# Two cross-attention layers on one core: scores in fp32 in place of three split products, and the last stage's root mean square moved into the clamp of the query lengths

## The reference

```python
def layer0(x, y, ...):
    xn, yn = layernorm(x, ln1_w, ln1_b), layernorm(y, ln2_w, ln2_b)
    q = (xn @ Wq)                       # 16 heads of 16
    k, v = split(yn @ Wkv)
    attn = softmax(q k^T * 16 ** -0.5)
    x = x + (attn v) @ Wproj + bproj
    h = gelu(layernorm(x, ln3_w, ln3_b) @ W1 + b1)
    return x + h @ W2 + b2
def layer1(x, enc, norm_w, wq, wkv, wout):
    xn = x * rsqrt(mean(x * x, -1) + 1e-5) * norm_w
    q = rotate(xn @ wq);  k, v = split(enc @ wkv);  k = rotate(k)
    q = q / maximum(norm(q), 1e-12);  k = k / maximum(norm(k), 1e-12)   # per head
    attn = softmax(q k^T * sqrt(16))
    return x + (attn v) @ wout
```

## Time and profile before

| | us |
|---|---|
| three runs | 385.35, 385.97, 391.71 |
| median | 385.97 |
| span of the profiled execution | 386.9 |

### The profile page before, as it was taken

One profiled execution on the slowest core, in us unless ns is written; L12 is line 12 of the kernel. 1 busy time (PEld: TensorE's weight loads), 2 busy tenths in 40 slices (PEclk: granted clock), 3 DMA queues, 4 the chain that ended last, 5 costly groups with the idle time before them and its releaser, 6 DMA issues.

```text
span 386.9 us, 11499 instructions
## 1 busy us (share of the span) xinstructions
PE 356.5 (92%) x4475; PEld 318.7 (82%) x4475; DVE 294.4 (76%) x654; ACT 239.3 (62%) x464; POOL 197.1 (51%) x177
## 2 busy tenths in 40 slices
PE   8998999999999989898999999978889989989974
PEld 5977888888888867798999998978778878878854
DVE  4799987989899773267755559467899999999752
ACT  2356677666677655815644476163877777777862
POOL 2474544554665611003331233248899998999810
PEclk9999999999999999999999999999999999999999
DMA  6853001110000000000000000000001001010001
GB/s 157 246 158 121 27 25 43 32 28 25 2 3 4 22 2 2 2 2 0 0 0 0 0 0 3 10 22 0 22 12 36 26 26 42 29 37 14 29 30 41
DMA packets 14432, 12.39 MB, mean 32 GB/s; under 512 B 2996, under 2 KB 13752, under 8 KB 14392
## 3 DMA queue, kind: packets, MB, share of 16 engines
q1 hardware_dynamic: 14384, 11.83, 10.4%
q10 hardware_dynamic: 8, 0.00, 0.0%
HBM read 9.73 MB, written 2.10 MB: 31 GB/s over the span
## 4 chain that ended last, share of the span: by engine, by line
PE 58%; issue 22%; DVE 10%; ACT 5%; POOL 4%; POOLq 0%; DVEq 0%; ACTq 0%
PE bank_qk L697 9%; PE banks_s L745 6%; PE bank_y L834 4%; PE bank_y L828 3%; PE banks_s L1032 3%; PE bank_t L800 3%; PE bank_qk L722 3%; PE bank_o L736 3%; PE bank_t L697 3%; PE bank_qk L726 3%; DVE row_max L1203 2%; POOL x_all L375 2%; PE bank_y L1052 2%; PE bank_o L1021 2%; PE bank_y L929 1%
## 5 line engine op out<-in xcount | busy, mean ns | idle before, releaser
L413 POOL TENSOR_TENSOR norm_inv<-norm_sq_min,minus_half 128x32 f32<-128x32 f32 x16 | 87.5, 5468 | 1.8 <-DVE norm_sq_min L1374 1.8
L576 ACT ACTIVATE W_s<-banks_s,b_cols 128x256 f32<-128x256 f32 x60 | 25.0, 469 | 41.3 <-PE banks_s L915 41.3
L342 POOL TENSOR_TENSOR masked<-qkT_r,halves_t 128x512 fp32r<-128x512 f32 x32 | 32.9, 1050 | 24.1 <-DVE qkT_r L1193 24.1
L477 ACT ACTIVATE PT<-banks_s 128x1024 f32<-128x1024 f32 x32 | 31.0, 1022 | 20.3 <-PE banks_s L782 18.3
L1203 DVE TENSOR_REDUCE row_max<-banks_s 128x8 f32<-128x1024 f32 x32 | 37.6, 1218 | 7.7 <-PE banks_s L745 7.7
L368 POOL TENSOR_TENSOR b_var_eps<-b_mean_var,eps_t 128x2 f32<-128x2 f32 x8 | 1.6, 197 | 69.1 <-DVE b_mean_var L1137 69.1
L915 PE MATMUL banks_s<-lnT_hi,W_hi 128*128 128x256 f32 x120 | 34.2, 285 | 0.0
L915 PE MATMUL banks_s<-lnT_hi,W_lo 128*128 128x256 f32 x120 | 33.9, 283 | 0.0
L915 PE MATMUL banks_s<-lnT_lo,W_hi 128*128 128x256 f32 x120 | 33.9, 283 | 0.0
L642 ACT ACTIVATE PT<-banks_s 128x1024 f32<-128x1024 f32 x32 | 31.1, 1024 | 4.1 <-PE banks_s L1032 4.1
L745 PE MATMUL banks_s<-masked,qkT_r 32*128 32x256 f32 x768 | 31.5, 294 | 1.6 <-DVE row_max L1203 1.3
(11 more groups left out here) (171 smaller groups left out, 1095.6 us busy)
## 6 DMA issues: line engine op xcount, KB each, us to landing
ctx_in<-in_ctx SPq DMA_DIRECT2D x32, 96.0 KB, 2.0
x_all<-in_x SPq DMA_DIRECT2D x16, 128.0 KB, 2.1
W_s<-in_L_xattn_W SPq DMA_DIRECT2D x2, 1024.0 KB, 6.4
out<-Wq_s SPq DMA_DIRECT2D x16, 128.0 KB, 1.8
Wq_s<-in_L_xattn_Wq SPq DMA_DIRECT2D x1, 256.0 KB, 3.0
Wkv_s<-in_L_xattn_Wkv SPq DMA_DIRECT2D x1, 256.0 KB, 3.2
Wproj_s<-in_L_xattn_Wproj SPq DMA_DIRECT2D x1, 256.0 KB, 4.2
wout_s<-in_L_xattn_wout SPq DMA_DIRECT2D x1, 256.0 KB, 3.0
```

Of the source, the lines that this page charges most:

```text
L342: nc.gpsimd.tensor_tensor(masked[:, r, 1, :, half, :], qkT_r[:, r, 1, :, :].bitcast(fp32), ones, ALU.mult)\
L413: nc.gpsimd.tensor_tensor(norm_inv[:, j, :], norm_sq_min[:, j, :], minus_half[:, :], ALU.pow)\
L477: nc.scalar.activation(PT[:, 2 * h:2 * h + 2, :], banks_s[:, 2 * h:2 * h + 2, :], ACT.Exp, scale=HD ** -0.5)\
L576: last = nc.scalar.activation(hT[:, m, :], (bank or bank_s[u])[:, 256 * k:256 * k + 256], ACT.Gelu, bias=b1_cols[:, m:m + 1])
```

## The change

- Queries and keys of both attention stages are kept as one fp32 copy (qkT, masked). score_terms and scores issue one fp32 product where three fp32r products stood: 8 per call in place of 24.
- The low parts go: queries_keys_lo, masked_lo, units_lo. In stage A the two masks are shared: ACT makes the one for the first half (masked_act), POOL the one for the second (masked_pool). In stage C ACT makes all three copies (units_out).
- In stage C x isn't normalised any more. inputs_c turns x_all itself. The mean square, scaled by EPS_L2 ** 2, is the lower limit in the clamp of the query lengths; keys keep the constant. POOL's power of it goes, and so do DVE's multiplication and rms_inv.
- New waits: mean_square on POOL's sum of two tiles before, POOL's sum on the clamp of two tiles before, the query clamp on POOL's sum, inputs_c on b_x (the MLP's residual) in place of norm_done. normed_c, units_T and scores wait for ACT's c_unit_T where they waited for DVE's c_unit_lo.
- TensorE's steps of stage C are all written out.

```diff
@@ -107,14 +107,15 @@
         minus_half = sb("minus_half", 128, 2 * H)
+        clamp_eps = sb("clamp_eps", 128, 1)
         x_all = sb("x_all", 128, NB, C1)
...
         inT = sb("inT", 128, 2, 4, TOK)
-        qkT_r = sb("qkT_r", 128, RING, 2, 4, TOK, dtype=fp32r)
-        masked = sb("masked", 128, RING, 2, 4, 2, TOK, dtype=fp32r)
-        pair = masked[:, :, :, 0:KT, :, :]
+        qkT = sb("qkT", 128, RING, 4, TOK)
+        masked = sb("masked", 128, RING, 4, 2, TOK)
+        pair = masked[:, :, 0:KT, :, :]
         vals = sb("vals", 128, 2, H, VW)
@@ -331,38 +332,37 @@
-            def masked_lo(t):
+            def masked_pool(t):
...
                     r = t % RING
-                    pool.wait_ge(a_qk_lo, t + 1)
+                    pool.wait_ge(a_qk_ready, t + 1)
                     wait(pool, a_shifted, t - 2)
-                    for half in range(2):
+                    for half in (1,):
                         ones = halves_t[:, half:half + 1].unsqueeze(2).broadcast_to([128, 4, TOK])
-                        nc.gpsimd.tensor_tensor(masked[:, r, 1, :, half, :], qkT_r[:, r, 1, :, :].bitcast(fp32), ones, ALU.mult)\
-                            .then_inc(a_masked_lo, 1)
+                        nc.gpsimd.tensor_tensor(masked[:, r, :, half, :], qkT[:, r, :, :], ones, ALU.mult).then_inc(a_masked_pool, 1)
@@ -400,16 +400,14 @@
                     pool.wait_ge(C["stats_ready"], t + 1)
-                    nc.gpsimd.tensor_tensor(mean_sq_eps[:, j, :], mean_sq[:, j, :], eps_t[:, 0:1], ALU.add)\
+                    wait(pool, c_norm_min, 2 * t - 2)
+                    nc.gpsimd.tensor_tensor(mean_sq_eps[:, j, :], mean_sq[:, j, :], clamp_eps[:, :], ALU.add)\
                         .then_inc(C["var_ready"], 1)
-                    pool.wait_ge(C["var_ready"], t + 1)
-                    nc.gpsimd.tensor_tensor(rms_inv[:, j, :], mean_sq_eps[:, j, :], minus_half[:, 0:1], ALU.pow)\
-                        .then_inc(C["rstd_ready"], 1)
...
                 if ok(t):
-                    pool.wait_ge(c_norm_min, t + 1)
+                    pool.wait_ge(c_norm_min, 2 * t + 2)
                     nc.gpsimd.tensor_tensor(norm_inv[:, j, :], norm_sq_min[:, j, :], minus_half[:, :], ALU.pow)\
@@ -438,21 +436,20 @@
-            def queries_keys_hi(t):
+            def queries_keys_T(t):
...
                     wait(act, a_shifted, t - 2)
-                    nc.scalar.activation(qkT_r[:, t % RING, 0, :, :], bank_qk[:, :].rearrange("p (a b) -> p a b", a=4), ACT.Copy)\
-                        .then_inc(a_qk_hi, 1)
-
-            def masked_hi(t):
-
-                if ok(t):
-                    act.wait_ge(a_qk_hi, t + 1)
-                    for half in range(2):
-                        nc.scalar.activation(masked[:, t % RING, 0, :, half, :], qkT_r[:, t % RING, 0, :, :].bitcast(fp32),
-                                             ACT.Copy, scale=halves_t[:, half:half + 1]).then_inc(a_masked_hi, 1)
+                    nc.scalar.activation(qkT[:, t % RING, :, :], bank_qk[:, :].rearrange("p (a b) -> p a b", a=4), ACT.Copy)\
+                        .then_inc(a_qk_ready, 1)
+
+            def masked_act(t):
+
+                if ok(t):
+                    act.wait_ge(a_qk_ready, t + 1)
+                    nc.scalar.activation(masked[:, t % RING, :, 0, :], qkT[:, t % RING, :, :], ACT.Copy, scale=halves_t[:, 0:1])\
+                        .then_inc(a_masked_act, 1)
@@ -597,7 +594,8 @@
                     wait(act, C["stats_ready"], t)
-                    nc.scalar.activation(x_sq[:, :], tile_of(t), ACT.Square, scale=C1 ** -0.5, accum_out=mean_sq[:, j, :])\
+                    wait(act, C["var_ready"], t - 1)
+                    nc.scalar.activation(x_sq[:, :], tile_of(t), ACT.Square, scale=EPS_L2 * C1 ** -0.5, accum_out=mean_sq[:, j, :])\
                         .then_inc(C["stats_ready"], 1)
@@ -622,16 +620,16 @@
-            def units_hi(t, j):
+            def units_out(t, j):
...
                     for half in range(2):
-                        nc.scalar.activation(pair[:, j, 0, :, half, :], bank_o[:, 0:C1].rearrange("p (a b) -> p a b", a=KT),
-                                             ACT.Copy, scale=halves_t[:, half:half + 1]).then_inc(c_unit_hi, 1)
-                    nc.scalar.activation(qkT_r[:, j, 0, KT:, :], bank_o[:, C1:].rearrange("p (a b) -> p a b", a=KT), ACT.Copy)\
-                        .then_inc(c_unit_hi, 1)
+                        nc.scalar.activation(pair[:, j, :, half, :], bank_o[:, 0:C1].rearrange("p (a b) -> p a b", a=KT),
+                                             ACT.Copy, scale=halves_t[:, half:half + 1]).then_inc(c_unit_T, 1)
+                    nc.scalar.activation(qkT[:, j, KT:, :], bank_o[:, C1:].rearrange("p (a b) -> p a b", a=KT), ACT.Copy)\
+                        .then_inc(c_unit_T, 1)
@@ -740,18 +738,17 @@
                 for tile in range(KT):
-                    for n, (a, b) in enumerate(HI_LO):
-                        for g in range(QUARTERS):
-                            last = mm(bank_s[g][:, 2 * TOK * tile:2 * TOK * (tile + 1)], qkT_r[quad(g), r, a, rows + tile, :],
-                                      masked[quad(g), r, b, columns + tile, :, :], start=n == 0 and (stop or tile == 0), stop=stop and n == 2)
-                            if stop and tile == KT - 1 and n == 2:
-                                last.then_inc(A["scores"], 1)
+                    for g in range(QUARTERS):
+                        last = mm(bank_s[g][:, 2 * TOK * tile:2 * TOK * (tile + 1)], qkT[quad(g), r, rows + tile, :],
+                                  masked[quad(g), r, columns + tile, :, :], start=stop or tile == 0, stop=stop)
+                        if stop and tile == KT - 1:
+                            last.then_inc(A["scores"], 1)
...
                 if ok(t):
-                    pe.wait_ge(a_masked_hi, 2 * t + 2)
-                    pe.wait_ge(a_masked_lo, 2 * t + 2)
+                    pe.wait_ge(a_masked_act, t + 1)
+                    pe.wait_ge(a_masked_pool, t + 1)
                     wait(pe, a_maxed, 2 * t)
@@ -985,11 +982,11 @@
                 if ok(t):
-                    pe.wait_ge(C["norm_done"], t + 1)
+                    pe.wait_ge(b_x, upto(t + 1))
                     pe.wait_ge(c_loaded[j], LOADED * (nth + 1))
...
                     for k in range(KT):
-                        nc.tensor.transpose(bank_t[:, 128 * k:128 * k + 128], xn[:, j, 128 * k:128 * k + 128], ident[:, :])
+                        nc.tensor.transpose(bank_t[:, 128 * k:128 * k + 128], tile_of(t)[:, 128 * k:128 * k + 128], ident[:, :])
                     for k in range(2):
@@ -1024,15 +1021,14 @@
                 if ok(t):
-                    pe.wait_ge(c_unit_lo, t + 1)
+                    pe.wait_ge(c_unit_T, 3 * t + 3)
                     wait(pe, C["exped"], 2 * t)
                     for half in range(KT):
-                        for n, (k, q) in enumerate(HI_LO):
-                            for g in range(NG):
-                                last = mm(bank_s[g][:, 2 * TOK * half:2 * TOK * (half + 1)], qkT_r[quad(g), j, k, KT + half, :],
-                                          pair[quad(g), j, q, half, :, :], start=n == 0, stop=n == 2)
-                                if half == KT - 1 and n == 2:
-                                    last.then_inc(C["scores"], 1)
+                        for g in range(NG):
+                            last = mm(bank_s[g][:, 2 * TOK * half:2 * TOK * (half + 1)], qkT[quad(g), j, KT + half, :],
+                                      pair[quad(g), j, half, :, :], start=True, stop=True)
+                            if half == KT - 1:
+                                last.then_inc(C["scores"], 1)
@@ -1056,7 +1052,7 @@
                     pe.wait_ge(C["on_ready"], t + 1)
-                    pe.wait_ge(c_unit_lo, upto(t + 3))
+                    pe.wait_ge(c_unit_T, 3 * upto(t + 3))
                     wait(pe, c_onT_lo, t)
@@ -1106,7 +1102,7 @@
             scores(0, 0)
-            pipeline(pe, step_c, 4, STEPS_C, peeled=8)
+            at(step_c, *range(4, STEPS_C))
@@ -1371,7 +1347,10 @@
                     dve.wait_ge(c_norm_sq, t + 1)
-                    v.tensor_scalar(norm_sq_min[:, j, :], norm_sq[:, j, :], EPS_L2 ** 2, None, ALU.max).then_inc(c_norm_min, 1)
+                    v.tensor_scalar(norm_sq_min[:, j, H:], norm_sq[:, j, H:], EPS_L2 ** 2, None, ALU.max).then_inc(c_norm_min, 1)
+                    dve.wait_ge(C["var_ready"], t + 1)
+                    v.tensor_scalar(norm_sq_min[:, j, 0:H], norm_sq[:, j, 0:H], mean_sq_eps[:, j, 0:1], None, ALU.max)\
+                        .then_inc(c_norm_min, 1)
@@ -1185,14 +1181,6 @@
-            def queries_keys_lo(t):
...
-                    v.tensor_tensor(qkT_r[:, r, 1, :, :], bank_qk[:, :].rearrange("p (a b) -> p a b", a=4),
-                                    qkT_r[:, r, 0, :, :].bitcast(fp32), ALU.subtract).then_inc(a_qk_lo, 1)
@@ -1334,13 +1317,6 @@
```

(31 more changed lines are left out.)

52 lines of the change are left out of this document (20 added, 32 removed).

## The result

The changed kernel takes 394.19 us in the median of four runs (392.7 to 395.61). Beside it the kernel before takes 387.32 (385.35 to 391.71). The ratio is 1.020, interval 1.014 to 1.026: between 1.4% and 2.6% slower, more than the 390.4 predicted, inside the range of 384.5 to 397. The runs of every kernel here lie in groups some 3 us apart, because the first scores start at 17.4 to 17.8 us in some executions and at 20.4 to 21.7 in others, and runs with a mean clock of 0.995 are longer again, of which the ratios leave out those over 1.5% above the fastest; so a median or a ratio can be off by 1 or 2 us, and what the change costs is read from traces, in stretches that begin with the first scores.

What follows compares the result with a forecast made beforehand. TensorE was taken to set the pace of both changed stages. Score calls +7.2, less 1.4, 0.3, 0.6 and 0.5 at the stages' ends, gave +4.4 us: 390.4 from a median of 385.97, range 384.5 to 397.

Steps and rivals of the forecast that it cites:

- Part 1: Scores in both stages: a call takes 1.07 for 0.92, or 0.97 for 0.82; 48 calls at 0.15 make +7.2 us.
- The bounds: Score call in fp32: from -0.27 us at the pace of one-pass records to +3.0 with no overlap of quadrants.
- B: Score calls: the quadrants lose their overlap, 2.2 us per call, +60 less some 3, about 443 us; chance 0.07.
- C: Score calls: quadrants overlap but three weight loads of 0.10 per call are exposed, +14, about 404 us; chance 0.08.
- E: Score calls: fp32 passes on 32 rows are cheaper than on 128, -13, about 370 us; chance 0.03.
- The start of the first stage: TensorE's wait of 1.34 for the second row maximum shrinks to nearly nothing, the 0.16 hole with it: -1.4 us.
- The end of the first stage: Holes of 0.20 and 0.72 before L820, behind DVE's residual, shrink by 0.15 each: -0.3 us.
- Both ends of the last stage: Start: waits for DVE shrink, -0.6 us; end: waits before L1062 go, norm chain is late next, -0.5 net.
- Parts 3 and 4: Last stage: mean square in the clamp, new waits met long before, 0; TensorE's loop written out, taken as 0.
- Rival D: Last stage: emptier DVE and ACT shorten the path to transposes; 0.45 per tile wins 5.4, time 385 us; chance 0.10.
- The base: Starting time of the sum: profiled span 386.9 us, median of three runs 385.97; +4.4 gives 391.3 profiled, 390.4 median.

## Why the prediction was right, and where it wasn't

- **Part 1** was right. A call was forecast at 1.07 for 0.92; it is 1.08 and 1.07. The shifted call, forecast at 0.97, is 0.78 with 0.20 more for the picks behind it, which comes to the same. 48 calls at 0.16 are 7.7 for the 7.2 forecast. The bounds were far apart (-0.27 and +3.0 a call; the 0.20 that stands beside the lower one is a slip, since 0.82 x 4/6 = 0.55 gives -0.27), and the row that I took between them, L800's fp32 records on separate parts of the array, was the right one.
- **Rivals B, C and E** are ruled out by the same call time. The rule of the Trainium skill, page "TensorE: Matmul & The Clock Gate", section "What overlaps and what doesn't", that matmuls start in program order, doesn't hold here: with one quadrant's products all ahead of the next one's, a call takes 1.09, not the 2.9 that I had estimated for that rule.
- **The start of the first stage** is the term that was mis-sized: -1.4 forecast. The holes there shrank by 0.8: 1.34 to 0.74, 0.16 to nothing, 0.34 to 0.16, and a new one of 0.15. The step that failed is "the maximum ends about 1.0 earlier": counted from the first scores it comes 0.07 earlier. The first maximum does come 0.21 earlier (1.29 behind the first scores, 1.50 before), but then the normalising beside POOL takes 0.79 more and eats the subtraction's 0.60. I took DVE's operations at their old durations, and didn't ask what moves beside them.
- **The end of the first stage**, -0.3 forecast, gave next to nothing: 0.20 went and 0.72 became 0.55, but a hole of 0.15 behind ACT's exponentials grew to 0.30 (142.11). Together the first stage was to cost 4.8 - 1.7 = 3.1; it costs 4.25.
- **Both ends of the last stage** were right in sum: 2.4 - 1.1 = 1.3 forecast, 1.1 measured (2.65 less 1.5 of clock). The waits before L1062 went. Next in line I had put the norm chain with its added clamp; the rows name another wait, holes of 0.71 and 0.17 before the unit transposes (L1018) for DVE's low part of the output (L1378).
- **Parts 3 and 4** at 0 were right for the time in the even run. The mean-square edit pays 1.0 only where the values' copy is moved as well.
- **Rival D** is out: the hole before L989 stays at 0.59 to 0.66. Its alternation, which I had thought TensorE's loop might cause, stays too with that loop written out.
- **The clock**, +1.5 in both traces of the changed kernel, was in no case of mine, although the 2.30 hole stood in the trace of before. By the mean clocks it isn't a price of the change: the kernel before has such runs as often. It makes two of the four runs of the result longer, and without it in them the median would still be some 393.4, past the own range that I gave the forecast (387.5 to 393), because the other two start late.
- **The base.** I put the profiled span of 386.9 0.9 above the median of 385.97. In the runs listed the time is 1.7 to 1.9 above the span (2.2 in one), so that execution took about 388.7 and belonged to a later-starting group than the median. The sum was against a profile; I then carried it over to a median of another group.

So the like-for-like change was 5.4 for 4.4 forecast: the mechanism and nearly the size. The traces add 1.5 of clock and come to 6.9; that the two medians also differ by 6.9 is luck, as they mix runs with early and late starts and with and without a fall.

What stays open is why the clock falls in one execution and not in another. In the traces it fell in all four with fp32 in the first stage and the 2.3 us hole, and in none of the three with the hole and without that fp32; but the mean clocks of the timed runs say that those kernels have falls too (35 of 72 for the kernel before, 3 of 12 with fp32 in the last stage alone), so seven traces make no rule. Nor is the 2.3 us hole needed: with the copy moved, three of four kernels still have such runs.

## What to carry to other kernels

Busy time taken from engines that aren't the bound is worth nothing as it stands, and here it was bought with 0.16 per call on the one that is. It becomes worth something once the waits between the engines are put in order: the same fp32 scores that cost 0.9 in the last stage gain 0.8 there when TensorE no longer waits for copies (one trace each), so decide such a trade stage by stage and after the order, not before. When an engine loses an operation in front of a critical one, price what moves up in its place and what then runs beside it. And before a fall of the clock in a trace is put down to a change, look at the mean clock of all timed runs of both kernels: here the kernel before had it in half of them.

## What I hadn't expected of the hardware

- Passes of fp32 products on the four 32-row quadrants overlap in whichever order the program has them: 16 records in 1.08 or 1.09 us. In terms of one quadrant, two fp32 products (four passes) cost 0.16 more than six one-pass ones.
- Two runs of one kernel can differ by 3 us before the first scores (17.42 and 20.40 in two traces of the changed kernel), while the rows give a clock of 1.00 in both. The difference arises behind 4.7 us, where two matmuls of 512 columns (L865) take 1.12 us in the one and 2.07 in the other.
- A DVE operation on 128x192 takes 0.41 us alone and 0.88 to 1.21 where a POOL operation runs beside it (16 records of one line in the trace of the changed kernel).
- The hardware loops of ACT and DVE together cost TensorE 0.11 to 0.24 us in a tile of 6.8, once nothing else covers them: 100.30 less 99.24, so 1.06 in the stage (one trace each).
